# A recurrent stage with two more inputs mixed ahead of their matmuls, and five element-wise steps on GpSimd

## The reference, cut to what matters

```python
for l in range(n_layer):
    h = layer_norm(x, ln1_w[l])
    prev = time_shift(h)
    k = jnp.einsum('btc,oc->bto', h * tm_mix_k[l] + prev * (1 - tm_mix_k[l]), tm_k_w[l])
    v = jnp.einsum('btc,oc->bto', h * tm_mix_v[l] + prev * (1 - tm_mix_v[l]), tm_v_w[l])
    r = jax.nn.sigmoid(jnp.einsum('btc,oc->bto', h * tm_mix_r[l] + prev * (1 - tm_mix_r[l]), tm_r_w[l]))
    wkv = wkv_scan(k, v, time_decay[l], time_first[l])
    x = x + jnp.einsum('btc,oc->bto', r * wkv, tm_o_w[l])
    h = layer_norm(x, ln2_w[l])
    prev = time_shift(h)
    kk = jnp.einsum('btc,fc->btf', h * cm_mix_k[l] + prev * (1 - cm_mix_k[l]), cm_k_w[l])
    vv = jnp.einsum('btf,of->bto', jnp.square(jax.nn.relu(kk)), cm_v_w[l])
    rr = jax.nn.sigmoid(jnp.einsum('btc,oc->bto', h * cm_mix_r[l] + prev * (1 - cm_mix_r[l]), cm_r_w[l]))
    x = x + rr * vv
return layer_norm(x, lnf_w)
```

## Time and profile before

| what | value |
|---|---|
| median of 3 runs | 4822.15 us (4816.67 to 4822.48) |
| the profiled execution, its own time | 4821.5 us |
| its span | 4819.6 us |
| PE busy over the span | 4417.6 us (92%) |
| DVE, ACT, POOL busy | 3409.0 (71%), 3123.7 (65%), 1471.2 (31%) |
| granted TensorE clock, mean | 0.962 |

### The profile page before, as it was taken

The page is one execution under the profiler, slowest core; times in us unless marked ns, Lnnn a source line. Parts: engine busy times, 40 slices in busy tenths (PEclk is TensorE's granted clock), DMA queues, the critical chain, the costliest instruction groups (busy, mean ns, idle before and its releaser), DMA issues. The chain is left out here.

```text
span 4819.6 us, 101682 instructions
## 1 busy us (share of the span) xinstructions
PE 4417.6 (92%) x37631; PEld 2907.1 (60%) x37631; DVE 3409.0 (71%) x5379; ACT 3123.7 (65%) x5579; POOL 1471.2 (31%) x1948
## 2 busy tenths in 40 slices
PE   8999788889969987999999999789979989999888
PEld 6767556557757764444444444467657767777665
DVE  7978777567763337889999995653349966666748
ACT  6878677567764336888888888653248844444356
POOL 3444354114407760000000000047734412222327
PEclk9999999889989999999999999899999999999999
DMA  3000000000021122000000000311130000000110
GB/s 106 3 2 3 2 1 1 1 13 3 3 63 51 52 69 84 1 1 1 1 1 1 1 1 20 110 31 53 53 104 3 3 2 1 1 2 1 57 55 36
DMA packets 124460, 119.57 MB, mean 25 GB/s; under 512 B 19536, under 2 KB 104528, under 8 KB 123216
## 3 DMA queue, kind: packets, MB, share of 16 engines
q1 hardware_dynamic: 106576, 77.38, 5.2%
q0 software_dynamic: 17408, 35.69, 2.6%
HBM read 82.60 MB, written 30.41 MB: 23 GB/s over the span
## 5 line engine op out<-in xcount | busy, mean ns | idle before, releaser
L2683 POOL TENSOR_TENSOR L_xattn_E<-L_xattn_E,L_xattn_rz 128x256 f32<-128x256 f32 x16 | 10.2, 635 | 1277.6 <-DVE L_xattn_rz L2839 1277.6
L1759 POOL DMA_INDIRECT L_ffn_xg<-L_ffn_xrows,L_ffn_take x272 | 263.2, 968 | 281.1 <-DVE L_ffn_take L2054 198.8
L1823 PEld LDWEIGHTS L_ffn_ps<-L_ffn_early_down,L_ffn_mT 128*128 128x128 f32 x1904 | 246.8, 191 | 105.8 <-issue 79.8
L1765 POOL DMA_INDIRECT L_ffn_yrows<-L_ffn_yo,L_ffn_put x272 | 268.3, 987 | 99.8 <-issue 59.8
L1803 PE MATMUL L_ffn_ps<-L_ffn_up,L_ffn_xT 128*128 x544 | 259.2, 559 | 19.6 <-issue 8.1
L2919 POOL TENSOR_TENSOR L_xattn_E<-L_xattn_E,L_xattn_rz 128x1024 f32<-128x1024 f32 x64 | 123.7, 1932 | 471.5 <-DVE L_xattn_rz L3139 471.5
L1823 PE MATMUL L_ffn_ps<-L_ffn_early_down,L_ffn_mT 128*128 x1904 | 259.0, 276 | 2.5 <-DVE L_ffn_yo L2084 1.3
L2263 PE MATMUL L_attn_ps<-L_attn_rl,L_attn_wcv 128*128 128x512 f32 x512 | 240.6, 592 | 0.0
L2247 PE MATMUL L_attn_ps<-L_attn_mix,L_attn_wck 128*128 128x512 f32 x512 | 240.6, 592 | 0.0
L1913 ACT ACTIVATE L_ffn_mT<-L_ffn_ps 128x512 f32<-128x512 f32 x136 | 81.2, 597 | 236.9 <-PE L_ffn_ps L1812 236.9
L2073 DVE TENSOR_TENSOR L_ffn_m<-L_ffn_b,L_ffn_ps 128x512 f32<-128x512 f32 x136 | 93.6, 688 | 188.4 <-PE L_ffn_ps L1803 188.4
(11 more groups left out here) (616 smaller groups left out, 13175.0 us busy)
## 6 DMA issues: line engine op xcount, KB each, us to landing
L_ffn_row_hot<-L_ffn_yrows SPq DMA_DIRECT2D x32, 256.0 KB, 3.0
L_ffn_col_hot<-L_ffn_yrows SPq DMA_DIRECT2D x32, 256.0 KB, 3.4
L_ffn_w<-in_L_ffn_e_W SPq DMA_DIRECT2D x32, 256.0 KB, 4.3
L_ffn_xrows<-L_ffn_xtok SPq DMA_DIRECT2D x42, 192.0 KB, 2.1
L_ffn_xg<-L_ffn_xrows,L_ffn_take POOLq DMA_INDIRECT x272, 2.5
L_ffn_yrows<-L_ffn_yo,L_ffn_put POOLq DMA_INDIRECT x272, 2.3
main_x<-in_xT SPq DMA_DIRECT2D x8, 512.0 KB, 7.5
main_ctx<-in_ctxT SPq DMA_DIRECT2D x4, 1024.0 KB, 11.5
```

Source lines behind the costliest of these rows:

```text
L1759: pool.indirect_dma_start(xg[t % RING][:], None, xrows, bass.IndirectOffsetOnAxis(ap=take[:, t:t + 1], axis=0)) \
L1765: pool.indirect_dma_start(yrows, bass.IndirectOffsetOnAxis(ap=put[:, t:t + 1], axis=0), yo[t % RING][:], None).then_inc(scattered[t % RING ...
L1823: g = pe.matmul(ps[1][:, 3, 0:P], mT[u][0:rows[a], a * P:(a + 1) * P], down[a][:, bass.ds(at, P)], start=(a == 0), stop=(a == FT - 1))
```

## The change

Second receptance and keys are mixed beforehand, as the first receptance already is: ACT scales the tokens, DVE adds the scaled shifted tokens, and PE has one matmul instead of two. `denominator`, `denominator_r`, `quotient` and `normal2` move from DVE to GpSimd, and the second half of `squared` moves from ACT to GpSimd, where it is a product of the tile with itself. The entry matmul and its copy go: in the first layer the steps read the input tensor itself (`before(m)`), which is centred by the layer norm ahead of it. `rold` and its four loads go, and `prepare` scales only the values' weights. All places of the table are set anew.

```diff
-            def enter(m):
-                pe.matmul(ps[:, 0, :], center[:], xres[:, m * CT:(m + 1) * CT], start=True, stop=True).then_inc(c_mm, 1)
...
             def keys(m):
-                pe.wait_ge(h1, m + 1)
+                pe.wait_ge(kmixed, m + 1)
...
-                mixed_in(2, 0, at(m)[0]).then_inc(k_mm, 1)
+                pe.matmul(ps[:, 2, :], now[:, 3 * at(m)[0], :], kmix[:], start=True, stop=True).then_inc(k_mm, 1)
...
             def receptance2(m):
-                pe.wait_ge(h2, m + 1)
+                pe.wait_ge(rmixed2, m + 1)
-                pe.matmul(ps[:, 7, :], rnow[:, l, :], hp2[:, :, 1:S1], start=True, stop=False)
-                pe.matmul(ps[:, 7, :], rold[:, l, :], hp2[:, :, 0:S], start=False, stop=True).then_inc(rr_mm, 1)
+                pe.matmul(ps[:, 7, :], rnow[:, l, :], rmix2[:], start=True, stop=True).then_inc(rr_mm, 1)
 
             def contract(m, half):
-                pe.wait_ge(sr, 2 * m + 1 + half)
+                pe.wait_ge((sra, srb)[half], m + 1)
...
+            def half_mixed_k(m):
+                act.activation(flat(kmix[:]), hp1[:, :, 1:S1], ACT.Identity, scale=tnow[:, l, 0:1]).then_inc(half_kmix, 1)
...
+            def half_mixed_r2(m):
+                act.activation(flat(rmix2[:]), hp2[:, :, 1:S1], ACT.Identity, scale=cnow[:, l, 1:2]).then_inc(half_rmix2, 1)
...
+        @block.gpsimd
+        def _(pool):
+            def denominator(m):
+                pool.wait_ge(g_ready, m + 1)
+                pool.wait_ge(den_ready, m + 1)
...
+                pool.tensor_tensor(flat(dn[:])[:, :, 1:S], ex[:, 0, :, 1:S], den[:, :, 0:S - 1], ALU.add).then_inc(low, 1)
+            def denominator_r(m):
+                pool.wait_ge(ln_low, m + 1)
+                pool.wait_ge(er_ready, m + 1)
+                pool.tensor_tensor(tokens(dl[:]), er[:], tokens(dl[:]), ALU.add).then_inc(low_r, 1)
+            def quotient(m):
+                pool.wait_ge(rec, m + 1)
+                pool.wait_ge(top, m + 1)
+                pool.tensor_tensor(gv[:], gv[:], tokens(dl[:]), ALU.mult).then_inc(wkv, 1)
+            def normal2(m):
+                pool.wait_ge(rs2, m + 1)
...
+                pool.tensor_tensor(hp2[:, :, 1:S1], flat(xw[:, at(m)[1]]), flat(rsb[:]), ALU.mult).then_inc(h2, 1)
+            def squared(m):
+                pool.wait_ge(relu, 2 * m + 2)
+                pool.tensor_tensor(rl[:, 2:4, :], rl[:, 2:4, :], rl[:, 2:4, :], ALU.mult).then_inc(srb, 1)
...
+            staggered(TURNS, PERIOD, (13.9, denominator), (19.5, denominator_r), (22.7, quotient), (30.4, normal2),
+                      (41.5, squared))
...
+            def mix_key(m):
+                dve.wait_ge(half_kmix, m + 1)
+                dve.scalar_tensor_tensor(flat(kmix[:]), hp1[:, :, 0:S], told[:, l, 0:1], flat(kmix[:]), ALU.mult, ALU.add) \
+                    .then_inc(kmixed, 1)
...
+            def mix_r2(m):
+                dve.wait_ge(half_rmix2, m + 1)
+                dve.scalar_tensor_tensor(flat(rmix2[:]), hp2[:, :, 0:S], cold[:, l, 1:2], flat(rmix2[:]), ALU.mult, ALU.add) \
+                    .then_inc(rmixed2, 1)
```

More of the change, by code:

```diff
@@ L2167, in at, with before @@
             return l, slice(n * CT, (n + 1) * CT)
+        def before(m):
+            l, tokens_of = at(m)
+            return (xres if l == 0 else xw)[:, tokens_of]
         def flat(t):
@@ L2292, in end_variance2 @@
                 pe.matmul(ps[:, 4, :], avg[:], rmix[:], start=True, stop=True).then_inc(evar2, 1)
[L2294 to L2300, removed]
+            interleaved((0, TURNS, 0, PERIOD, (
+                            (-0.5, variance1), (21.2, keys), (30.9, values), (37.7, receptance), (50.8, output),
+                            (56.3, variance2), (62.2, lambda m: hidden(m, 0)), (61.4, receptance2),
+                            (67.2, lambda m: hidden(m, 1)), (76.3, lambda m: contract(m, 0)),
+                            (76.5, lambda m: contract(m, 1)), (77.5, centred))),
+                        (TURNS, NT, END, END_PERIOD, ((8.8, variance1), (21.5, end_sum), (25.3, end_variance2))))
         @block.scalar
@@ L2306, in _ @@
             act.activation(rate[:], col[:, :, 4], ACT.Exp).then_inc(rate_exp, 1)
[L2308 to L2310 removed]
             def square1(m):
[L2313 to L2315 removed]
+                if m >= NT:
                     act.wait_ge(xc3, m - NT + 1)
@@ L2318, in square1 @@
                     act.wait_ge(var1_mm, m)
-                act.activation(sqa[:], xw[:, at(m)[1]], ACT.Square).then_inc(sq1, 1)
+                act.activation(sqa[:], before(m), ACT.Square).then_inc(sq1, 1)
             def rstd1(m):
@@ L2390, in rectified @@
                 act.activation(rl[:, 2 * half:2 * half + 2, :], ps[:, 5:7, :], ACT.Relu).then_inc(relu, 1)
-            def squared(m, half):
-                act.wait_ge(relu, 2 * m + 1 + half)
-                act.activation(rl[:, 2 * half:2 * half + 2, :], rl[:, 2 * half:2 * half + 2, :], ACT.Square).then_inc(sr, 1)
+            def squared(m):
+                act.wait_ge(relu, 2 * m + 1)
+                act.activation(rl[:, 0:2, :], rl[:, 0:2, :], ACT.Square).then_inc(sra, 1)
             def exp_rr(m):
@@ L2623, in _ @@
             interleaved((0, TURNS, 0, PERIOD, (
[L2624 to L2630 removed]
+                            (7.0, normal1), (21.9, mix_r), (10.5, mix_key), (29.7, clamp_r), (22.0, running_max), (23.3, exponents_ab),
+                            (25.6, exponent_g), (26.8, clamp_g), (25.7, weighted), (28.6, scan_den), (34.6, scan_num),
+                            (34.6, bonus), (34.8, numerator), (44.6, residual1), (55.2, mix_k), (54.2, mix_r2), (57.2, clamp_rr),
+                            (71.1, gated), (73.6, residual2))),
+                        (1, NL - 1, PERIOD, PERIOD, ((-8.5, prepare),)),
+                        (TURNS, NT, END, END_PERIOD, ((9.8, normal1), (26.9, end_close))))
 def padded_attention(nc, k, d, col, early, ahead):
```

95 lines of the change are left out of this document (41 added, 54 removed).

## The result

The changed kernel takes 4928.73 us (median of 4 runs, 4927.41 to 4930.24) against 4819.41 for the kernel before, measured with it: a ratio of 1.0227, 95% interval 1.0209 to 1.0245. It is slower, as forecast, by 109 us where 181 were forecast; 4928.7 lies in the range of 4885 to 5070.

A forecast was written before the change was run, and what follows sets the result against it. PE was taken as the bound, without a gap at 16.31 us a turn; the change would make turns 19.4. 4821.5 - 13.7 + 63 x 3.1 (195.3) = 5003 us, chance 0.50; range 4885 to 5070.

The forecast's parts named there:

- the round trips: Two waits of PE on other engines each turn, before the contracts and before `centred`: 1.79 and 1.05 us.
- 18.1 us if DVE is in time for `gated`: Laid-out steady turn with both PE waits, ACT's queue (0.30) and the late exponent (0.35), before any lateness of DVE at `gated`.
- the second round trip: PE's contracts wait for `variance2`'s result because ACT's `squared` stands behind `rstd2`: 1.79 us a turn.
- the 2 to 3.7 us that were given as the sign: Sign in the changed profile: DVE's scans, held by GpSimd, take this long, well over their 1.21 us.
- the lighter rival: Only DVE's plain products wait for GpSimd, not exponent or scans: a turn of 17.7, 4896 us; chance 0.25.
- the exponent's hold: DVE's exponent waits for `quotient` on GpSimd, so `exp_ab` and everything after it come 0.35 us later.
- the failed step: The numerator's scan on DVE waits for `normal2` and `denominator` on GpSimd, to 16.72 us into the turn.
- 3.1 us a turn: Forecast lengthening of the steady turn, 19.4 us instead of 16.3; over 63 steps 195.3 us.
- the entry: In the first 16 turns, 16 entry matmuls of 0.858 us leave PE: 13.7 us gained whole.
- 10 either way: Fill and drain around the steady turns left as they are, with an uncertainty of 10 us, half a turn.
- the forecast's own 4959 to 5041: Range without rivals: 4959 if the numerator precedes `denominator_r` (a turn of 18.7), 5041 with another 0.6 of waits.
- the rival at 0.17: PE's stands lower its clock to half, 1.7 us each: 5057 us if every second turn, 5110 if every; chance 0.17.

The follow-up runs named there:

- Experiment 1: Changed kernel with one place in ACT's list moved: `squared` of the turn before stands ahead of `rstd2` instead of behind it; 4863.88 us.
- experiment 8: Changed kernel's steps on the same engines, with all four engines' lists in a new order; 4775.88 us against 4817.37 for the kernel before, ratio 0.992.
- experiment 7: Changed kernel with `quotient` moved back from GpSimd to DVE, behind `exponents_ab`; 4988.79 us.
- Experiment 5: Changed kernel with one wait more: the numerator's scan on DVE also waits for `denominator` on GpSimd; 4977.43 us.
- experiment 11: Kernel before with only the entry matmul and its copy taken out; 4808.25 us against 4817.37, ratio 0.9983.
- Experiments 2: Changed kernel with the keys on PE moved to between the contracts and `centred`, instead of ahead of the contracts; 4993.08 us.
- 6: Changed kernel with `square2` ahead of `ln_rr` on ACT instead of behind it; 4943.50 us.
- experiments 3: Changed kernel with the five GpSimd steps put back on DVE and ACT, at the places where they ran; 4952.55 us.
- 4: Changed kernel with only the second half of `squared` back from GpSimd to ACT, right behind the first half; 4945.38 us.

## Why the prediction was right in direction and too high

*Right: PE's list and the round trips.* The layout with "18.1 us if DVE is in time for `gated`" is the measured turn, piece by piece. From `centred` to `variance2`: 9.73 + 0.35 = 10.08 laid out, 10.07 measured (2512.76 - 2502.69). From `variance2` to the contracts: 1.72 of work and 1.79 of waiting, 3.51; measured 3.51. From there to `centred`: 3.43 + 1.05 = 4.48; measured 4.55. Experiment 1 takes the second round trip away and the turn falls by 1.00; experiment 8 covers both, and most holds end with it: the loss becomes a gain.

*Right: GpSimd holds up DVE, mixes and scans included*, for which only products had rows. The Trainium skill, "SBUF — State Buffer", section "Who interferes with whom", says this for any DVE instruction with two SBUF inputs; the trace agrees (1250, 2381 and 1756 ns). Of the two scans only the numerator's was held, and for less than the 2 to 3.7 us that were given as the sign. So the lighter rival fell as a mechanism: its 17.7 and 4896 left out the exponent's hold. That the hold is worth 0.35 to the turn rests on the piece to `variance2` fitting; experiment 7 couldn't isolate it.

*Wrong, the failed step: "`normal2`, ready since 12.47, goes first and `denominator` right behind it, to 15.64. The numerator's scan waits until then, to 16.72."* In the timeline the scan is issued at 2515.94 while `normal2` runs; `normal2` ends at 2516.62, and the scan goes next. `denominator`, issued at 2516.58, waits for the scan instead (2.18 us). The scan ends at 15.01 behind `centred`, not at 16.72; `numerator` at 16.61, ahead of `denominator_r`, not at 18.65; and DVE stands 0.78 us before `gated`. So DVE is in time, and of the 3.1 us a turn 1.3 don't exist. The mistake was to read the one row of 10.32 us behind five GpSimd products as the rule for any two that are queued. The row of 1.45 us beside it showed the other outcome, since there too a GpSimd product stood right behind the one that ran:

```profile
4750.92 1.45 DVE L3777 TENSOR_TENSOR main_x<-main_x,L_combine_rs 128x512 f32<-128x512 f32 x1
4751.79 2.37 POOL L3586 TENSOR_TENSOR L_combine_E<-L_combine_E,L_combine_rz 128x1024 f32<-128x1024 f32 x1
```

Of the eight held products of L3777 in the kernel before, seven waited for one GpSimd product (1.04 to 1.49 us) with the next one queued, and one for all five. Experiment 5 forces the order: 18.88 instead of 18.13. The other 0.5 us of the 1.3 are pieces that were taken too long: counted from the `centred` at 2487.49, the scan ends at 16.48 in that run (16.72 laid out) and `numerator` at 18.24 (18.65).

*Too large: the entry.* 13.7 us were counted; experiment 11 shows 9.4 in the steps. Only eleven steps were longer (17.17 to 17.27); the other five entry matmuls lie ahead of the first `centred`, where their end brought 0.6. That is 10.0 in all.

*Left out: the ends.* The last four steps cost 7.1 us more and the fill 5.3, the part behind 4.5 less, 7.9 in all; "10 either way" holds, and what makes the ends longer stays open.

*The sum with the measured sizes:* 4821.5 + 107.4 - 9.6 + 7.1 + 5.3 - 4.5 = 4927.2; the profiled execution took 4927.4. The pieces are read from the same two traces, so this shows that no piece is missing, and not why each is as long as it is.

*Luck in the number.* The measured 4928.7 lies below the forecast's own 4959 to 5041, and nearer to the 4896 of the lighter rival, whose mechanism fell, than to 5003. The stated range holds it because it was drawn to take that rival in.

*The clock* stayed at 1.00 in the steady turns of the changed kernel, against the rival at 0.17. Experiments 2, 6 and 7 show its price of 1.7 us in 38, 8 and 22 of the 63 steps. A longer or shifted stand of PE doesn't bring it by itself: with 1.53 us before the contracts in experiments 3 and 4, and 1.60 before `centred` in 5, the granted clock was 1.00 from 2168 to 2920.

## What to carry to other kernels

Taking work off the engine that was the bound paid here only when the lists were laid out again, so that each round trip to another engine had independent work behind it: the same steps gave 4928.7 us in one order and 4775.9 in another. When one engine's instructions can hold up another's, look at every row of such a meeting and not at the longest one, ask which of the two was issued first, and only then add up waits. And where the engine that gains room starts to stand, look at its clock.
